# Moving the basis lots to fixed stretches of each block of eight windows

## The reference

```
layer 0: h1 = x@Wn + bn; neigh = segment_sum(h1[src], dst)
         out = relu(concat([neigh + img@Wim + bim, h1], 1) @ Wap + bap)   # img: attention over 36 rows
layer 1: two RGCN layers, each: w[r] = sum over 30 bases of att[r, b] * basis[b]    # basis is [30, 512, 512]
         msg = sigmoid(x[col] @ gate_w[r]) * x[col] @ w[r], r = edge_type
         out = segment_sum(msg, row) + x@root + bias
layer 2: five GIN layers, each relu(((1+eps)*h + segment_sum(h[src], dst)) @ W + b), then log_softmax
layer 3: segment_sum((x@weight)[src] * edge_weight, dst) + bias
```

## Time and profile before

| | |
|---|---|
| runs of the kernel | 1826.46, 1818.31, 1824.29 us |
| profiled execution, own time | 1819.87 us |
| its span | 1818.0 us |
| TensorE busy | 1755.0 us, 97% of the span |
| VectorE busy | 874.1 us, 48% |
| ScalarE busy | 594.6 us, 33% |

### The profile page before, as it was taken

How to read it: one execution, slowest core, us unless ns; L and a number is a source line. 1 busy time by engine, 2 the same in 40 slices (tenths; PEclk the granted TensorE clock), 3 DMA queues, 4 the chain that set the end, 5 groups by cost and what they waited for, 6 DMA issues and landing times.

```text
span 1818.0 us, 22292 instructions
## 1 busy us (share of the span) xinstructions
PE 1755.0 (97%) x7318; PEld 849.4 (47%) x7318; DVE 874.1 (48%) x1890; ACT 594.6 (33%) x1232; POOL 10.8 (1%) x36
## 2 busy tenths in 40 slices
PE   5989888999999999999999999999999999999998
PEld 3556555533334444444444444444544444444444
DVE  7888787489885312112222224334253443594123
ACT  2555444566876311222110001232323323232000
POOL 1000000000000000000000000000000000000000
PEclk9999999999999999999999999999999999999999
DMA  7999979810302401000011116300000010021111
GB/s 182 273 254 263 267 230 237 327 36 1 145 24 81 168 2 46 0 1 23 0 47 35 35 35 241 147 0 30 1 0 30 1 41 1 1 84 56 35 47 47
DMA packets 45781, 157.80 MB, mean 87 GB/s; under 512 B 7686, under 2 KB 9630, under 8 KB 37094
## 3 DMA queue, kind: packets, MB, share of 16 engines
q1 hardware_dynamic: 43792, 146.95, 26.6%
q10 hardware_dynamic: 1878, 9.44, 1.4%
HBM read 120.71 MB, written 35.65 MB: 86 GB/s over the span
## 4 chain that ended last, share of the span: by engine, by line
PE 82%; DVE 7%; issue 3%; DMA 3%; DVEq 3%; ACT 1%; POOL 0%; POOLq 0%
PE psum L1556 31%; PE psum L1570 31%; PE psum L1797 7%; DMA hs<-in_L_gnn_basis 3%; PE psum L1747 2%; PE psum L1484 2%; PE psum L1451 2%; PE psum L1644 2%; PE psum L1631 1%; PE psum L1483 1%; PE psum L1522 1%; DVEq L702 1%; DVE hs L723 1%; DVE xt L723 1%; DVEq L723 1%
## 5 line engine op out<-in xcount | busy, mean ns | idle before, releaser
L1570 PE MATMUL psum<-hs,adj 128*128 128x512 f16 x2880 | 636.2, 379 | 0.0
L1556 PE MATMUL psum<-wb,xt 128*128 128x512 f32 x1056 | 457.7, 593 | 0.0
L1570 PEld LDWEIGHTS psum<-hs,adj 128*128 128x128 f16 x2880 | 281.2, 98 | 330.7 <-issue 11.0
L1556 PEld LDWEIGHTS psum<-wb,xt 128*128 128x128 f32 x1056 | 198.7, 190 | 245.3 <-issue 243.6
L1335 ACT ACTIVATE ua<-ua 128x512 f32<-128x512 f32 x60 | 37.9, 631 | 314.7 <-DVE ua L1113 181.0
L1109 DVE SCALAR_TENSOR_TENSOR vt<-psum,scl,xt 128x512 f32<-128x512 f32 x60 | 44.8, 746 | 192.7 <-PE psum L1570 192.7
L1044 DVE TENSOR_TENSOR vt<-psum,adj 128x512 f32<-128x512 f32 x24 | 16.6, 692 | 249.3 <-PE psum L1556 249.3
L1556 PE MATMUL psum<-adj,xt 128*128 128x512 f32 x288 | 130.1, 594 | 0.0
L1797 PE MATMUL psum<-hs,adj 128*128 128x512 f32 (+1 forms) x312 | 123.8, 559 | 0.0
L1323 ACT ACTIVATE lnst<-lnst,bcol 128x1 f32<-128x1 f32 x24 | 7.1, 295 | 280.1 <-DVE lnst L1022 270.5
L1036 DVE SCALAR_TENSOR_TENSOR hs<-psum,gates,hs 128x512 f16<-128x512 f32 x48 | 33.8, 747 | 120.9 <-ACT hs L1358 120.9
(11 more groups left out here) (256 smaller groups left out, 1880.7 us busy)
## 6 DMA issues: line engine op xcount, KB each, us to landing
hs<-in_L_gnn_basis SPq DMA_DIRECT2D x38, 960.0 KB, 10.3
adj<-in_L_gnn_basis SPq DMA_DIRECT2D x26, 960.0 KB, 11.8
aw_scratch<-xt ACTq DMA_DIRECT2D x12, 768.0 KB, 10.1
adj<-aw_scratch SPq DMA_DIRECT2D x1, 9216.0 KB, 37.1
x_scratch<-adj SPq DMA_DIRECT2D x24, 256.0 KB, 2.3
hs<-x_scratch SPq DMA_DIRECT2D x24, 256.0 KB, 2.6
ts_scratch<-adj SPq DMA_DIRECT2D x2, 2304.0 KB, 19.5
as_scratch<-adj SPq DMA_DIRECT2D x1, 4608.0 KB, 16.8
```

Of the source, the lines that this page charges most:

```text
L1556: x = pe.matmul(psum[:, bank, :], xt[:, i, k, :], w[:, k, :], start=first and k == 0, stop=last and k == 3)
L1570: x = pe.matmul(psum[:, i % 2 + (4 * half if own else 0), :], adj[:, m, j, P * i:P * i + P], hs[:, t, half, j, :], start=n == 1 or (own an ...
```

## The change

The window of each basis lot is picked by its place q = u % 8 in the block, and the lot's number by counting the basis lots so far:

```
-            if u % 3 != 2:
-                n = 2 * (u // 3) + u % 3
+            at_q = (0, 2, 4, 5, 6) if s == BLOCKS - 2 else (0, 2, 4, 6, 7) if s % 3 else (0, 2, 4, 5, 6, 7)
+            if q in at_q:
+                n = len([what for what in side if what[0] == "basis"])
                 here.append(("basis", n // (CH // 2), n % (CH // 2)))
```

## The result

| | before | after |
|---|---|---|
| median of 10 runs each | 1823.45 us (1815.44 to 1826.66) | 1830.18 us (1825.15 to 1839.02) |
| ratio | | 1.0043, 95% interval 1.0024 to 1.0062 |
| profiled execution, own time | 1819.87 us | 1834.26 us |

The changed kernel is slower by 0.43%, some 7.8 us, within the half per cent that was set as the limit of "same", and the forecast of 1828 us is 2 us short of the median.

The account below looks back on a forecast made before the run. VectorE's pace, round trips for second tiles and nearly full DMA engines take turns in bounding the build, two-buffer turns its end. Tail 5.6, body -2, double windows 0: +3.6 us, 1828 on the median's scale; range of 8 in 10, 1818 to 1838.

Parts of the forecast that it names:

- Only the build can change: Build, 21 to 318 us: the change acts only there; what ends late or early is passed on behind it.
- The body gives 2 us: Windows 0 to 77: later places shrink the 5.22 us wait at window 59; -2 us, bounds 0 and -4.
- the prediction's own sign: Window 72 reached 1 to 4 us earlier if right; if later than before, the body's term has the wrong sign.
- Double windows and second tiles cost 0: Build: fewer windows with both kinds of lot, some waits for second tiles longer, some shorter; 0, bounds -2 and +2 us.
- The tail costs 5.6 us, 7.5 at most: Windows 76 to 94: B51 two windows later, B63 ends at 321.2 instead of 315.6; +5.6 us, bounds +3.1 and +7.5.
- the walk: Tail, B51 to B63 followed lot by lot with the old window times; B63 ends at 321.2 us, +5.6 us.
- turns: Two-buffer tail: multiply, load the follower, multiply; each about 8.6 + 1.1 + 0.15 = 9.8 us.
- Rival 1: Tail: TensorE's clock falls after waits, two more stretches at 1.7 us each, body +1.5; +10.5 us, 1835 us; chance 0.20.
- The rival's +1.5 us in the body: Rival 1's body term: the body loses 1.5 us because the early loads come late.
- The transfer rule of the Trainium skill: Tail: 2.0 us plus bytes over 436 GB/s, 4.3 us a chunk, turn about 5.5 us; 1822 us, within rival 2's chance.
- rival 2: Build faster: window 59's stall goes (-3.8), second-tile waits -2, tail only +3.1; -2.7 us, 1821.5; chance 0.11.
- Rival 3: Build bound by bytes, same 61 MB at the same rate, places don't matter; 1824 us; chance 0.13.

Follow-up runs that it names:

- body alone: Basis lots as after the change up to window 72, as before from window 73 on; ratio to the kernel before 1.0000 (0.9985 to 1.0015).
- half loads: Half of each chunk's load left out, from B4 on: changed kernel 0.9982, kernel before 0.9958; for B54 to B63 only: 1.0006 and 0.9969.
- tail alone: Basis lots as before up to window 72, as after the change from window 73 on; ratio to the kernel before 1.0041 (1.0020 to 1.0061).
- the pairs with shorter turns: Old and new order compared under third buffer, half loads for B54 to B63, and half loads from B4 on; new order behind by 5.5, 6.7, 4.4 us.
- third buffer: Last twelve chunks turn over three buffers in place of two: ratio to the kernel before 1.0015 in the changed kernel, 0.9985 in the kernel before.
- lots earlier: Kernel before with basis lots added in windows 2 and 5, none in 93 and 94, four buffers up to B55; ratio 1.0051.
- its first part: Kernel before with only B49 to B53 placed as after the change, then on as before; ratio 1.0037 (1.0021 to 1.0052).

## Why the prediction was right, and where it was off

1. **Only the build can change.** Right: from Wf to the end 1492.8 to 1496.6 us in all fourteen traces.
2. **The body gives 2 us.** Its price stands within what can be measured: mean window 72 of 241.8 against 244.3 us, -2.4, each single trace being good to some 2 us, and the body alone at 1.0000, whose interval reaches 2.7 us either way. A gain of 2 us is neither shown nor excluded by this. Its reason was read too finely. The 5.22 us wait at window 59 belonged to one execution; the same order showed 3.78 us at window 32 in another. What is stable is that the chunks come late by a little somewhere. In the two profiled executions this term had the other sign (+3.6), since the kernel before was caught at its fastest body, 240.5. So by the prediction's own sign (window 72 later than before) this term would be wrong; the sign asked more of a single trace than it can tell. Wf, forecast at 325 to 328 us, came at 338.2; what the body doesn't give of that is the tail's (4).
3. **Double windows and second tiles cost 0.** Mis-sized: with half loads, where only two chunks are late (1.8 us in all), the new order costs +1.6 us by window 72 and 3.3 behind it, of which at least 1.5 without a late chunk. The bounds of 2 us held for the body; for the whole, 3.1 to 4.9 us lie above them. Lots in 84 to 88 stand in five windows running.
4. **The tail costs 5.6 us, 7.5 at most.** The places were right: every wait before B53, B57, B58, B59 and B63 came, and the walk is within 0.6 us of the tail alone up to B57. The size was too small: 7.5 us by the ratio of the tail alone, 10.9 in its trace, which took 6.1 us more than the median. The steps that came out short in the trace are the last ones. B59's chunk took 9 us in the walk and 10.2 in the trace, beside a row store (+1.2); the chain is then 1.4 us behind at B61 and 2.7 at B63; and from B63 to Wf it took 9.8 us in the tail alone, 8.6 in the changed kernel and not 7.2, most of it the lower clock after B63's wait. And the walk put the whole 5.6 us down to turns; the pairs with shorter turns leave it open whether they carry so much.
5. **Rival 1, the lower clock.** Its condition came in the trace, two such stretches more than before: three in the changed kernel's tail (275 to 279, 302 to 306 and 329 to 333 us) against one; in the tail alone two, the second lasting from 325 to 336 us, with lots of 1.87 and 1.94 us. At the rival's 1.7 us each, two more are 3.4 us, which the forecast had left out; with the walk's 5.6 that makes 9.0, beside 11.8 - 2.0 = 9.8 us in the changed kernel's trace without the wait before B48. No run shows that price by itself. The rival's +1.5 us in the body did not come. The forecast had counted these as either or; the measured 1830 lies between its 1828 and that rival's 1835. The Trainium skill, "TensorE: Matmul & The Clock Gate", section "HAM oscillation", says that waits on loads between bursts bring the clock down; the traces agree for the waits of 2.86 and 2.90 us, but not for each wait: after 1.54 us before B53 the changed kernel's counts ran at half speed, while B57 after 2.28 us, or 1.89 in the tail alone, was followed by none.
6. **The transfer rule of the Trainium skill** ("DMA: Bandwidth & Descriptors", "Anatomy of one DMA"), by which a turn would fit into two windows, fell: no full chunk in the changed kernel's tail landed in less than 6.8 us. That section gives its fit for transfers that GpSimd issues; the chunks are loaded by SP, so the prediction carried it over to another kind of issue.
7. **Rivals 2 and 3.** No gain came, against rival 2. Rival 3, by which the bytes alone set the end, doesn't fit either: at the same bytes the tail alone is 0.41% slower.

Sum by the ratios: 0 for the body alone and +7.5 for the tail alone, against 7.8 us for the whole change; the traces give -2.4 and +10.9. The forecast of +3.6 had the sign and the place right and about half of the size. That 1828 lies only 2 us from the median is partly luck: the median of the kernel before came out 0.8 us lower than the one that the forecast was put on.

Still open: how the tail's loss parts. Half loads leave 4.4 to 6.7 us between the two orders, the third buffer 5.5 of 7.8. No run parts the three causes (a turn longer than two windows, TensorE's backlog before a second tile, and the clock), and each can bring about the next: a late chunk makes TensorE wait, the clock falls, and the counts before a second tile end later.

## What to carry to other kernels

With a ring of two buffers, compare the distance from a use to the next use of the same buffer with the whole turn, load plus use, and the load's time read where it runs beside others. Where a chain of turns is the end of a stage, a shift of one link is neither absorbed nor added to the next; walk the chain to its end, and add the price of the lower clock where waits of TensorE stand close together. To learn what such a turn costs, compare both orders with the turn relieved, not one of them with the other's full time: here a third buffer took 5.1 us from one order but 2.7 from the other too. And where the DMA engines are nearly full, moving the uses earlier need not gain: here it cost 0.51%.

## What the runs showed of the hardware

- Loads of the same 120 x 8 KB from HBM took 6.6 us at the least (in the kernel before, at 303.1 us, with another one under way for the second half of it), mostly 8.0 to 8.8 with two buffers, and 7.7 to 18.4 (median 12.5; changed kernel 9.3 to 18.9, median 16.1) from 60 to 240 us with four; half of the bytes took 4.5 us at the median.
- At DMA shares of 0.94 to 0.98 the rate was anything from 225 GB/s (lots earlier, 50 to 75 us) to 305 (kernel before with three buffers, 175 to 200 us) in stretches of 25 us, and the same order reached window 72 between 240.5 and 246.8 us in six executions. That spread is larger than most effects here; with half loads the runs of the kernel before's order lay within 1.9 us (1815.34 to 1817.19, five runs) instead of 11.2 (ten runs).
- In the tails TensorE's lower clock level came after waits of 1.54 to 2.90 us and lasted some 3.5 us in the changed kernel and before, and some 10 us once in the tail alone and once in its first part; with half loads throughout neither kernel's trace shows one between 245 and 324 us.
